# A retention kernel on eight cores: the gated products move from VectorE to GpSimd, the row scale to ScalarE

## The chip, the cores and the metric

The kernel runs on all eight cores of one Trainium2 chip. Each core works on two sequences of its own; the cores exchange nothing. The metric is the device time of the slowest core, in microseconds.

## What is computed

One layer on x of shape 16 x 2048 x 1024. The attention part is a retention with four heads (q and k 256 wide, v 512 wide), with a norm and a gate per head:

```python
xn = layernorm(x)
q, k = rotary(xn @ Wq, xn @ Wk);  v = xn @ Wv          # per head
# per chunk of tokens, gamma per head:
attn  = (q_c @ k_c.T) * decay
o_c   = attn @ v_c + (q_c * cross_q) @ S
S     = gamma**chunk * S + (k_c * cross_k).T @ v_c
o     = o * rsqrt(mean(o*o) + 1e-5) * gn_weight        # per token and head
s     = (o * silu(xn @ Wg)) @ Wo
out   = x + s * silu(ffn(xn))                          # ffn: silu(gate) * up, down
```

The kernel takes chunks of 128 tokens, 16 per sequence.

## The kernel before

For each of its two sequences a core runs two phases with a barrier between them: `_phase_attn` (LayerNorm, and then for each of four heads the projections and the recurrence) and `_phase_wo_ffn` (the product with Wo, then the FFN). Engines have their own instruction streams and wait for each other by counting semaphores (`WG(engine, semaphore, value)`).

**Projections of head h.** TensorE computes q and k (transposed), v, and the gate, in 48 groups of eight matmuls; ScalarE evacuates each group (`eraw`, `vtb`, and for the gate a Silu into `gtmp`); VectorE does the rotary products and multiplies the gate by the norm's weight into `ggb` (L508), 16 slots of 512 columns, one per chunk. GpSimd issues the 16 loads of the head's v and gate weights; it waits only for the matmuls of the head before, so they run under that head's recurrence.

**Recurrence of head h**, loop over c = 0 to 15. TensorE's order in a chunk is: `og_tr(c - 5)`, four transposes (L522) of a finished chunk from `og_sb` into the one PSUM tile `ogT_ps`; the matmuls of `o_ps` (L556, and L562 with the state S); two matmuls of the state's increment `U_ps` (L570); then `at_kt(c + 2)`, which computes the scores of chunk c + 2 (L533) and transposes its k (L540) into `kt_ps`. The k transposes wait until `ktok(c + 1)` has been written, by semaphore `sKT`. ScalarE's order is: `og_evac(c - 6)` (L636, `ogT_ps` to `og_st`), `ktok(c)` (L647, `kt_ps` scaled by `ck_sb`), the copy of `o_ps` into `o_win` (L654, four slots), and the square of `o_ps` with its row sum in `ss_sb` (L658). VectorE's order is: the two halves of the S update (L599), the mask of chunk c + 2 (L587), and after every fourth chunk, which ends a window w = c // 4, the norm of the window: eleven small instructions for the rsqrt (L611 and `_quake_rsqrt`, the last is L107) and four products of 128 x 512 (L623) that multiply `o_win` by the row's rsqrt and by `ggb` into `og_sb`. SyncE sends each `og_st` to DRAM.

The first write into a slot of `o_win` in a new window waits for the product that read it:

```python
WG(sc, sOGv.h, b["ogv"] + c - 3)
sc.copy(out=o_win[:, (c % 4) * 512:(c % 4 + 1) * 512],
        in_=o_ps[:, par * 512:(par + 1) * 512]).then_inc(sOE.h, 1)
```

After the loop TensorE does `og_tr` of chunks 11 to 15 and ScalarE `og_evac` of chunks 10 to 15. The next head's first matmul stands behind the last of these transposes in TensorE's stream.

Of the kernel before, what the change touches and what calls it, by code (L numbers as in the profile page):

```python
# [22 lines left out]
NCH = T // CH  # L23
# [89 lines left out]
def build_nc():  # L113
# [40 lines left out]
    rr_sb = A("rr_sb", [128, 4], F32)  # L154
# [170 lines left out]
def _phase_attn(G, s):  # L325
# [26 lines left out]
    o_win = SB("o_win", [128, 4 * 512], BF16)  # L352
    og_sb = SB("og_sb", [128, 4 * 512], BF16)
    og_st = SB("og_st", [128, 2 * 512], BF16)
    sq_scr = SB("sq_scr", [128, 512], F32)
# [9 lines left out]
    with es, nc.Block() as blk:  # L365
# [16 lines left out]

        for h in range(NHEADS):
            b = dict(tp=sTp.n, pe=(b_h0["pe"] if h == 0 else sPE.n), rp=sRP.n,
                     gt=sGT.n,
                     ta=sTa.n, tk=sTk.n, to=sTo.n, tu=sTu.n, tog=sTog.n,
                     at=sAT.n, st=sS.n, rr=sRr.n, ot=sOT.n, ogv=sOGv.n,
                     kt=sKT.n, oe=sOE.n, oge=sOGE.n,
                     sp=[sSPs[0].n, sSPs[1].n])

            @blk.gpsimd
            def _(g, h=h, b=b):
                WG(g, sTp.h, b["tp"])
                for k in range(KC):
                    g.dma_start(out=wv_sb[:, k * 512:(k + 1) * 512],  # L395
                                in_=G.wv_d[k * 128:(k + 1) * 128, h * 512:(h + 1) * 512]
                                ).then_inc(sWH.h, 16)
                    g.dma_start(out=wg_sb[:, k * 512:(k + 1) * 512],
                                in_=G.wgt_d[k * 128:(k + 1) * 128, h * 512:(h + 1) * 512]
                                ).then_inc(sWH.h, 16)  # L400
                sWH.n += 16 * 2 * KC
            wl_h = sWH.n

# [65 lines left out]
            def _(v, h=h, b=b):  # L469
# [36 lines left out]
                for c in range(NCH):  # L506
                    WG(v, sPE.h, b["pe"] + 32 + c + 1)
                    ins = v.tensor_mul(out=ggb[:, c * 512:(c + 1) * 512],  # L508
# [5 lines left out]
            def _(te, h=h, b=b):  # L514
# [33 lines left out]
                for c in range(NCH):  # L548
# [4 lines left out]
                    WG(te, sOE.h, b["oe"] + c - 1)  # L553
                    WG(te, sOT.h, b["ot"] + c - 1)
# [27 lines left out]
            def _(v, h=h, b=b):  # L582
# [11 lines left out]
                for c in range(NCH):  # L594
# [13 lines left out]
                    if c % 4 == 3:  # L608
                        WG(v, sOT.h, b["ot"] + 4 * w + 4)
# [6 lines left out]
                        _quake_rsqrt(v, G.rr_sb[:, 0:4], G.qk3[:, 0:4],  # L616
                                     G.qk1, G.qk2, sem=sRr)
                        v.drain()
                        WG(v, sOE.h, b["oe"] + 4 * w + 4)
                        for cc in range(4):  # L620
                            cw = 4 * w + cc
                            WG(v, sTog.h, b["tog"] + cw - 3)
                            ins = v.scalar_tensor_tensor(  # L623
                                out=og_sb[:, (cw % 4) * 512:(cw % 4 + 1) * 512],
                                in0=o_win[:, cc * 512:(cc + 1) * 512],
                                scalar=G.rr_sb[:, cc:cc + 1],
                                in1=ggb[:, cw * 512:(cw + 1) * 512],
                                op0=ALU.mult, op1=ALU.mult)
                            sOGv.inc(ins)

            @blk.scalar
            def _(sc, h=h, b=b):
# [6 lines left out]

                for c in range(NCH):  # L640
                    par = c % 2
                    w = c // 4
                    if c >= LAG + 1:
                        og_evac(c - LAG - 1)
# [8 lines left out]
                    WG(sc, sOGv.h, b["ogv"] + c - 3)  # L653
                    sc.copy(out=o_win[:, (c % 4) * 512:(c % 4 + 1) * 512],  # L654
# [3 lines left out]
                    sc.activation(out=sq_scr[:, :],  # L658
# [4 lines left out]
                                  ).then_inc(sOT.h, 1)  # L663
                    sOT.n += 1
# [4 lines left out]
            def _(sy, h=h, b=b):  # L669
# [7 lines left out]
                if h == H - 1:  # L677
                    WG(sy, sSPs[0].h, sSPs[0].n)
                    WG(sy, sSPs[1].h, sSPs[1].n)

# [300 lines left out]
```

## Time and profile before

| | us |
|---|---|
| median of 3 runs (2972.0 to 2981.34) | 2979.19 |
| the profiled execution | 2977.59 |
| its span, slowest core (core 0) | 2975.8 |
| spans of the eight cores | 2946.6 to 2975.8 |
| TensorE matmuls busy | 2346.8 (79%) |
| VectorE busy | 804.6 (27%) |
| ScalarE busy | 804.5 (27%) |
| GpSimd busy | 295.2 (10%) |

The profile is that of the slowest core in one execution. The span goes from its first to its last instruction; what lies around it makes the difference to the execution's time. Busy shares are averages over phases of different kinds: in the FFN TensorE is nearly always busy, in the recurrences every engine waits for others. A row's bracket tells how long the engine had been idle before the instruction and what released it. The granted clock is that of TensorE as a share of 2.4 GHz; it has two levels, 1.2 and 2.4 GHz.

### The profile page before, as it was taken

The page shows a single profiled execution, that of the slowest core. Times are in us where ns is not written, and L with a number is a line of the kernel's source. Part 1 is how long each engine was busy: PE and PEld are TensorE (multiplying, and loading weights), DVE is VectorE, ACT ScalarE, POOL GpSimd, SP SyncE. Part 2 cuts the span into 40 slices and gives each one's busy share as a digit, 9 for nine tenths or more (in the row PEclk, how much of TensorE's full clock was granted, in tenths as well). Part 3 has the DMA queues.
Part 4 walks back from the last instruction along what each step waited for, and adds up shares of the span by engine and source line. Part 5 has one row for each costly group of instructions (what it writes and reads, how often), then busy time and mean ns, then how long its engine had stood idle before and what let it go on. Part 6 is the DMA issues. An engine that isn't in the chain of part 4 may idle for free. (4 is left out here: it accounts for less than half of the span.)

```text
span 2975.8 us, 32058 instructions; the slowest of 8 cores (2946.6 to 2975.8 us)
## 1 busy us (share of the span) xinstructions
PE 2346.8 (79%) x10608; PEld 1039.5 (35%) x10608; DVE 804.6 (27%) x1745; ACT 804.5 (27%) x1560; POOL 295.2 (10%) x436
## 2 busy tenths in 40 slices
PE   1395968778459999999914969697883699999999
PEld 0142423333124444444402424243331244444444
DVE  2325343352300111211223243534423001121112
ACT  2534343333301111111045343434332011111110
POOL 2001010100110221021020100101003002201210
PEclk9597978778679999999956969687785899999999
DMA  9102020200293675475380110202003937755753
GB/s 177 59 1 50 8 41 16 34 24 1 56 184 110 82 74 93 111 78 57 113 176 30 19 39 1 47 11 40 19 4 79 180 113 72 74 96 103 74 50 120
DMA packets 295311, 202.03 MB, mean 68 GB/s; under 512 B 210544, under 2 KB 259824, under 8 KB 295024
## 3 DMA queue, kind: packets, MB, share of 16 engines
q0 software_dynamic: 234240, 96.50, 28.3%
q1 hardware_dynamic: 60912, 103.48, 11.0%
q8 instruction: 92, 1.51, 0.2%
q14 instruction: 67, 0.55, 0.1%
HBM read 254.45 MB, written 41.94 MB: 100 GB/s over the span
## 5 line engine op out<-in xcount | busy, mean ns | idle before, releaser
L842 PE MATMUL P<-xnT,wgu 128*128 128x512 bf16 x1536 | 353.2, 384 | 27.9 <-DMA wgu<-fuw 18.9
L898 DVE TENSOR_TENSOR hT<-sg_sc,P 128x1024 bf16<-128x1024 bf16 x96 | 117.2, 1221 | 923.8 <-PE P L853 923.8
L853 PE MATMUL P<-xnT,wgu 128*128 128x512 bf16 x1536 | 347.2, 379 | 0.0
L869 PE MATMUL P<-wd_sb,hT 128*128 128x512 bf16 x1536 | 332.2, 379 | 6.8 <-DVE hT L898 6.8
L773 PE MATMUL P<-wo_sb,ogl 128*128 128x512 bf16 x1024 | 234.9, 394 | 98.1 <-DMA wo_sb<-wo 72.0
L881 ACT ACTIVATE sg_sc<-P 128x1024 bf16<-128x1024 f32 x96 | 98.3, 1024 | 565.8 <-PE P L842 565.7
L842 PEld LDWEIGHTS P<-xnT,wgu 128*128 128x128 bf16 x1536 | 148.1, 99 | 224.3 <-issue 61.0
L435 PE MATMUL U_ps<-wv_sb,xnT 128*128 128x512 bf16 x1024 | 222.3, 379 | 0.0
L435 PE MATMUL U_ps<-wg_sb,xnT 128*128 128x512 bf16 x1024 | 222.3, 379 | 0.0
L869 PEld LDWEIGHTS P<-wd_sb,hT 128*128 128x128 bf16 x1536 | 150.0, 98 | 188.9 <-issue 8.6
L599 DVE SCALAR_TENSOR_TENSOR S<-S,U_ps 128x512 bf16<-128x512 bf16 x240 | 154.0, 683 | 224.0 <-PE U_ps L570 224.0
L853 PEld LDWEIGHTS P<-xnT,wgu 128*128 128x128 bf16 x1536 | 150.3, 98 | 181.2
L315 PE MATMUL lnps<-id_sb,ln_xn 128*128 128x128 bf16 x256 | 30.3, 291 | 201.6 <-DMA wk_sb<-wk 105.3
L540 PE MATMUL kt_ps<-id_sb,kT 128*128 128x128 bf16 x256 | 43.2, 264 | 182.3 <-ACT ktok L647 182.3
L773 PEld LDWEIGHTS P<-wo_sb,ogl 128*128 128x128 bf16 x1024 | 102.6, 101 | 229.9 <-issue 118.2
L819 POOL DMA_DIRECT2D wgu<-fgw x92 | 80.4, 874 | 966.2 <-PE P L853 966.2
L654 ACT CAST o_win<-o_ps 128x512 bf16<-128x512 f32 x128 | 75.0, 586 | 319.1 <-PE o_ps L562 223.1
L421 PE MATMUL U_ps<-xnT,wq_sb 128*128 128x512 bf16 x512 | 144.9, 453 | 14.3 <-ACT xnT L275 14.3
L508 DVE TENSOR_TENSOR ggb<-gtmp,gw_sb 128x512 bf16<-128x512 bf16 x128 | 54.5, 426 | 373.0 <-ACT gtmp L462 373.0
L435 PEld LDWEIGHTS U_ps<-wg_sb,xnT 128*128 128x128 bf16 x1024 | 100.2, 98 | 120.8
L435 PEld LDWEIGHTS U_ps<-wv_sb,xnT 128*128 128x128 bf16 x1024 | 100.2, 98 | 120.8
L395 POOL DMA_DIRECT2D wv_sb<-wv x64 | 40.4, 631 | 1007.2 <-PE U_ps L435 1007.2
(85 smaller groups left out, 2225.7 us busy)
## 6 DMA issues: line engine op xcount, KB each, us to landing
wgu<-fgw POOLq DMA_DIRECT2D x96, 256.0 KB, 4.7
wgu<-fuw POOLq DMA_DIRECT2D x96, 256.0 KB, 5.3
ln_x<-x SPq DMA_DIRECT2D x32, 512.0 KB, 6.3
og_spill<-og_st SPq DMA_DIRECT2D x128, 128.0 KB, 1.7
ogl<-og_spill SPq DMA_DIRECT2D x128, 128.0 KB, 2.6
xc_sb<-x SPq DMA_DIRECT2D x32, 512.0 KB, 4.0
out<-o_sb SPq DMA_DIRECT2D x32, 512.0 KB, 5.1
wd_sb<-fdw POOLq DMA_DIRECT2D x48, 256.0 KB, 39.5
```

What stands on the lines that cost most here:

```text
L421: ins = te.matmul(U_ps[:, par * 512:(par + 1) * 512], wsb[:, k * D + (2 * h + d) * 128: k * D + (2 * h + d + 1) * 128], G.xnT[:, k * T + n ...
L435: ins = te.matmul(U_ps[:, par * 512:(par + 1) * 512], G.xnT[:, k * T + c * 128:k * T + (c + 1) * 128], wsb[:, k * 512:(k + 1) * 512], star ...
L508: ins = v.tensor_mul(out=ggb[:, c * 512:(c + 1) * 512], in0=gtmp[:, (c % 2) * 512:(c % 2 + 1) * 512], in1=G.gw_sb[:, h * 512:(h + 1) * 512])
L599: ins = v.scalar_tensor_tensor(out=Sb[(c + 1) % 2][:, d * 512:(d + 1) * 512], in0=Sb[c % 2][:, d * 512:(d + 1) * 512], scalar=float(GAMMAS ...
L654: sc.copy(out=o_win[:, (c % 4) * 512:(c % 4 + 1) * 512], in_=o_ps[:, par * 512:(par + 1) * 512]).then_inc(sOE.h, 1)
L773: ins = te.matmul(ps[:, n * 512:(n + 1) * 512], ogl[:, (m % 2) * 2048 + k * 128: (m % 2) * 2048 + (k + 1) * 128], wo_sb[:, k * D + n * 512 ...
L819: g.dma_start(out=wgu[:, par * 1024:(par + 1) * 1024] .rearrange("p (k j) -> p k j", j=128), in_=G.fgw_d[m].rearrange("(k p) j -> p k j", ...
L842: ins = te.matmul(fgps[:, n * 512:(n + 1) * 512], wgu[:, par * 1024 + k * 128: par * 1024 + (k + 1) * 128], G.xnT[:, k * T + tok0 + n * 51 ...
L853: ins = te.matmul(fups[:, n * 512:(n + 1) * 512], wgu[:, 2048 + par * 1024 + k * 128: 2048 + par * 1024 + (k + 1) * 128], G.xnT[:, k * T + ...
L869: ins = te.matmul(ps[:, n * 512:(n + 1) * 512], hT[:, k * 1024 + mc * 128:k * 1024 + (mc + 1) * 128], wd_sb[:, k * D + n * 512:k * D + (n ...
L881: sc.activation(out=sg_sc[:, (m % 2) * 1024:(m % 2 + 1) * 1024], in_=fgps[:, :], func=AF.Silu, scale=Q127).then_inc(sFE.h, 1)
L898: ins = v.tensor_mul(out=hT[:, m * 1024:(m + 1) * 1024], in0=sg_sc[:, (m % 2) * 1024:(m % 2 + 1) * 1024], in1=fups[:, :])
```

## The change

Three things happen to a window's norm. The rsqrt stays on VectorE and now writes one of two halves of `rr_sb`. The multiplication by the row's rsqrt goes to ScalarE: `ot_batch(w)` makes four scaled copies of 128 x 512 from `o_win` into a new tile `ot8`. It stands at the head of chunk 4w + 5, ahead of `og_evac` and `ktok` of that chunk, and for the last window after the loop, ahead of the remaining `og_evac`s. The multiplication by `ggb` goes to GpSimd (`emit_og_gp`), whose products wait for `ot8` and write `og_sb`; in GpSimd's stream they stand behind the weight loads of the next head. `o_win` has six slots instead of four and its copy waits for no product. `sOE` now counts the copy and the square (two per chunk) and `sOT` the scaled copies. The square's scratch output goes to `scr`. VectorE waits before each write of `ggb` for the product of the head before. The capture of the counts `b` moves behind GpSimd's code of the head.

```diff
-    rr_sb = A("rr_sb", [128, 4], F32)
+    rr_sb = A("rr_sb", [128, 8], F32)
...
-    o_win = SB("o_win", [128, 4 * 512], BF16)
+    o_win = SB("o_win", [128, 6 * 512], BF16)
+    ot8 = SB("ot8", [128, 4 * 512], BF16)
...
-    sq_scr = SB("sq_scr", [128, 512], F32)
...
+        def emit_og_gp(g, bo):
+            for j in range(NCH):
+                WG(g, sOT.h, bo["ot"] + j + 1)
+                WG(g, sGT.h, bo["gt"] + j + 1)
+                WG(g, sTog.h, bo["tog"] + j - 3)
+                ins = g.tensor_mul(
+                    out=og_sb[:, (j % 4) * 512:(j % 4 + 1) * 512],
+                    in0=ot8[:, (j % 4) * 512:(j % 4 + 1) * 512],
+                    in1=ggb[:, j * 512:(j + 1) * 512])
+                sOGv.inc(ins)
...
                 sWH.n += 16 * 2 * KC
+                if bprev is not None:
+                    emit_og_gp(g, bprev)
...
                     WG(v, sPE.h, b["pe"] + 32 + c + 1)
+                    WG(v, sOGv.h, b["ogv"] + c - 15)
...
-                    WG(te, sOE.h, b["oe"] + c - 1)
-                    WG(te, sOT.h, b["ot"] + c - 1)
+                    WG(te, sOE.h, b["oe"] + 2 * c - 2)
...
-                        WG(v, sOT.h, b["ot"] + 4 * w + 4)
+                        WG(v, sOE.h, b["oe"] + 8 * w + 8)
+                        WG(v, sOT.h, b["ot"] + 4 * w - 4)
...
-                        _quake_rsqrt(v, G.rr_sb[:, 0:4], G.qk3[:, 0:4],
-                                     G.qk1, G.qk2, sem=sRr)
-                        v.drain()
-                        WG(v, sOE.h, b["oe"] + 4 * w + 4)
-                        for cc in range(4):
-                            cw = 4 * w + cc
-                            WG(v, sTog.h, b["tog"] + cw - 3)
-                            ins = v.scalar_tensor_tensor(
-                                out=og_sb[:, (cw % 4) * 512:(cw % 4 + 1) * 512],
-                                in0=o_win[:, cc * 512:(cc + 1) * 512],
-                                scalar=G.rr_sb[:, cc:cc + 1],
-                                in1=ggb[:, cw * 512:(cw + 1) * 512],
-                                op0=ALU.mult, op1=ALU.mult)
-                            sOGv.inc(ins)
+                        _quake_rsqrt(v, G.rr_sb[:, wp * 4:wp * 4 + 4],
+                                     G.qk3[:, 0:4], G.qk1, G.qk2, sem=sRr)
...
+                def ot_batch(wb):
+                    WG(sc, sRr.h, b["rr"] + wb + 1)
+                    for cc in range(4):
+                        j = 4 * wb + cc
+                        WG(sc, sOGv.h, b["ogv"] + j - 3)
+                        sc.activation(out=ot8[:, (j % 4) * 512:(j % 4 + 1) * 512],
+                                      in_=o_win[:, (j % 6) * 512:(j % 6 + 1) * 512],
+                                      func=AF.Identity,
+                                      scale=G.rr_sb[:, (wb % 2) * 4 + cc:
+                                                    (wb % 2) * 4 + cc + 1]
+                                      ).then_inc(sOT.h, 1)
+                        sOT.n += 1
...
+                    if c % 4 == 1 and c >= 5:
+                        ot_batch(w - 1)
                     if c >= LAG + 1:
                         og_evac(c - LAG - 1)
...
-                    WG(sc, sOGv.h, b["ogv"] + c - 3)
-                    sc.copy(out=o_win[:, (c % 4) * 512:(c % 4 + 1) * 512],
+                    sc.copy(out=o_win[:, (c % 6) * 512:(c % 6 + 1) * 512],
...
-                    sc.activation(out=sq_scr[:, :],
+                    sc.activation(out=scr[:, 0:512],
...
-                                  ).then_inc(sOT.h, 1)
-                    sOT.n += 1
+                                  ).then_inc(sOE.h, 1)
+                    sOE.n += 1
+                ot_batch(NCH // 4 - 1)
                 for c in range(NCH - LAG - 1, NCH):
                     og_evac(c)
...
+            bprev = b
+
+        @blk.gpsimd
+        def _(g, bprev=bprev):
+            emit_og_gp(g, bprev)
```

## Rows read from the trace of the kernel before

**Rows 1.** The profile page, its first line.
```profile
span 2975.8 us, 32058 instructions; the slowest of 8 cores (2946.6 to 2975.8 us)
```

**Rows 2.** The page's chain that ended last: shares of the span by line.
```profile
PE P L869 6%; PE P L842 5%; PE P L853 4%; DMA wgu<-fuw 2%; POOL wgu L819 0%; DVE hT L898 0%; DVE t_sb L906 0%; DVE o_sb L910 0%; ACT g_sc L888 0%; POOLq L42 0%; DVEq L42 0%; ACTq L42 0%; DVEq L909 0%
```

**Rows 3.** Head 1's recurrence, 387-467: PE, PEld, DVE, ACT, POOL busy; PEclk, DMA share, GB/s.
```profile
387.00:467.00 80.00, 47.32 (x206) 19.84 (x204) 41.33 (x108) 33.74 (x80) 7.77 (x15) 0.61 0.27 50
```

**Rows 4.** Timeline, a plain chunk step: start, length, engine, line, [idle before <-releaser].
```profile
416.19 0.59 ACT L654 CAST o_win<-o_ps 128x512 bf16<-128x512 f32 x1 [2.40 <-PE o_ps L562]
...
417.72 0.50 ACT L647 ACTIVATE ktok<-kt_ps,ck_sb 128x256 bf16<-128x256 bf16 x1
...
418.36 0.37 PE L540 MATMUL kt_ps<-id_sb,kT 128*128 128x128 bf16 x2 [1.25 <-ACT ktok L647]
...
418.59 0.58 PE L522 MATMUL ogT_ps<-id_sb,og_sb 128*128 128x128 bf16 x4
...
420.62 0.59 ACT L654 CAST o_win<-o_ps 128x512 bf16<-128x512 f32 x1 [2.41 <-PE o_ps L562]
```

**Rows 5.** Timeline, the same step at the full TensorE clock.
```profile
434.73 0.59 ACT L654 CAST o_win<-o_ps 128x512 bf16<-128x512 f32 x1 [1.77 <-PE o_ps L562]
...
438.53 0.59 ACT L654 CAST o_win<-o_ps 128x512 bf16<-128x512 f32 x1 [1.77 <-PE o_ps L562]
```

**Rows 6.** Timeline, evacuations around the first ends of a window of four.
```profile
397.70 0.59 ACT L654 CAST o_win<-o_ps 128x512 bf16<-128x512 f32 x1 [2.26 <-PE o_ps L562]
...
401.45 0.59 ACT L654 CAST o_win<-o_ps 128x512 bf16<-128x512 f32 x1 [2.21 <-PE o_ps L562]
...
411.76 0.59 ACT L654 CAST o_win<-o_ps 128x512 bf16<-128x512 f32 x1 [3.28 <-PE o_ps L562]
...
426.10 0.59 ACT L654 CAST o_win<-o_ps 128x512 bf16<-128x512 f32 x1 [3.45 <-DVE og_sb L623]
...
430.93 0.59 ACT L654 CAST o_win<-o_ps 128x512 bf16<-128x512 f32 x1 [2.80 <-PE o_ps L562]
...
448.76 0.59 ACT L654 CAST o_win<-o_ps 128x512 bf16<-128x512 f32 x1 [2.79 <-PE o_ps L562]
```

**Rows 7.** Groups by line: busy us, mean ns | idle before, releasers.
```profile
L898 DVE TENSOR_TENSOR hT<-sg_sc,P 128x1024 bf16<-128x1024 bf16 x96 | 117.2, 1221 | 923.8 <-PE P L853 923.8
...
L654 ACT CAST o_win<-o_ps 128x512 bf16<-128x512 f32 x128 | 75.0, 586 | 319.1 <-PE o_ps L562 223.1 <-DVE og_sb L623 87.3 <-PE o_ps L556 8.7
...
L647 ACT ACTIVATE ktok<-kt_ps,ck_sb 128x256 bf16<-128x256 bf16 x128 | 62.7, 490 | 0.1
...
L508 DVE TENSOR_TENSOR ggb<-gtmp,gw_sb 128x512 bf16<-128x512 bf16 x128 | 54.5, 426 | 373.0 <-ACT gtmp L462 373.0
...
L540 PE MATMUL kt_ps<-id_sb,kT 128*128 128x128 bf16 x256 | 43.2, 264 | 182.3 <-ACT ktok L647 182.3
...
L302 ACT ACTIVATE ln_xn<-ln_x,lb_sb,lr_sb 128x1024 bf16<-128x1024 f32 x32 | 37.1, 1230 | 7.9 <-DVE lb_sb L265 7.9
```

**Rows 8.** Timeline of ScalarE in the LayerNorm: four scaled writes in a run.
```profile
132.39 4.63 ACT L302 ACTIVATE ln_xn<-ln_x,lb_sb,lr_sb 128x1024 bf16<-128x1024 f32 x4
```

**Rows 9.** Timeline, end of head 1 and start of head 2.
```profile
457.01 0.59 ACT L654 CAST o_win<-o_ps 128x512 bf16<-128x512 f32 x1 [1.80 <-PE o_ps L562]
...
458.08 0.59 ACT L636 COPY og_st<-ogT_ps 128x512 bf16<-128x512 bf16 x1
...
459.54 0.59 ACT L636 COPY og_st<-ogT_ps 128x512 bf16<-128x512 bf16 x1 [0.88 <-PE ogT_ps L522]
...
460.71 0.16 DVE L107 TENSOR_TENSOR rr_sb<-rr_sb,qk 128x4 f32<-128x4 f32 x1
...
462.16 0.59 PE L522 MATMUL ogT_ps<-id_sb,og_sb 128*128 128x128 bf16 x4 [2.77 <-DVE og_sb L623]
...
466.55 0.58 PE L522 MATMUL ogT_ps<-id_sb,og_sb 128*128 128x128 bf16 x4 [0.88 <-ACT og_st L636]
...
466.93 8.31 PE L421 MATMUL U_ps<-xnT,wq_sb 128*128 128x512 bf16 x25
```

More of the change, by code:

```diff
@@ L381, in _ @@
             sWQK.n += 16 * 2 * KC
-        for h in range(NHEADS):
[L384 to L389, printed above, removed]
+        def emit_og_gp(g, bo):
[8 more added lines that the diff above has]
+                sOGv.inc(ins)
+        bprev = None
+        for h in range(NHEADS):
+            tp_gate = sTp.n
             @blk.gpsimd
-            def _(g, h=h, b=b):
-                WG(g, sTp.h, b["tp"])
+            def _(g, h=h, tp_gate=tp_gate, bprev=bprev):
+                WG(g, sTp.h, tp_gate)
                 for k in range(KC):
@@ L401, in _ @@
                 sWH.n += 16 * 2 * KC
+                if bprev is not None:
+                    emit_og_gp(g, bprev)
             wl_h = sWH.n
+            b = dict(tp=sTp.n, pe=(b_h0["pe"] if h == 0 else sPE.n), rp=sRP.n,
+                     gt=sGT.n,
+                     ta=sTa.n, tk=sTk.n, to=sTo.n, tu=sTu.n, tog=sTog.n,
+                     at=sAT.n, st=sS.n, rr=sRr.n, ot=sOT.n, ogv=sOGv.n,
+                     kt=sKT.n, oe=sOE.n, oge=sOGE.n,
+                     sp=[sSPs[0].n, sSPs[1].n])
             @blk.tensor
```

## The prediction, made before the result was known

> **What bounds the kernel now.** I read the page first. Its span is 2975.8 us [rows 1]; the execution took 2977.59 us, 1.8 us more, and against the median of the runs shown (2979.19 us) it is 0.05% low, so I make the sum on 2977.59. The chain that ended last has only lines of the FFN in it [rows 2]; it does not reach back to the attention phase, where every changed line stands. But each sequence runs its phases one after the other with a barrier between them, and inside the attention phase the recurrence of head h stands before the projections of head h+1 on TensorE. So what the recurrence of one head gains or loses, the total gains or loses, eight times (four heads, two sequences). I read head 1 of the first sequence. In its 80 us TensorE is busy 47.3 us, VectorE 41.3, ScalarE 33.7, GpSimd 7.8, and the granted clock is 0.61 [rows 3]. No engine is full: the recurrence is bound by a loop of waits.
>
> The timeline shows the loop. A plain step, from one `o_win` evacuation to the next, is 4.43 us (416.19 to 420.62) [rows 4]. ScalarE evacuates `o_ps`, squares it, evacuates a transposed chunk (`og_st`) and writes `ktok`, whose start is 1.53 us after the first. TensorE can transpose the next pair of k chunks only when that `ktok` is written (L540 starts at 418.36, after "ACT ktok"), then come `og_tr` (418.59) and the three matmuls of `o_ps`, whose end starts the next evacuation. The grouped row of L540 says the same of all heads: TensorE idles 182.3 us before it, all for `ktok` [rows 7]. So everything that ScalarE does ahead of `ktok` lies on the path, though ScalarE is idle half of the time. At the full clock the step is 3.80 us [rows 5].
>
> Twice per window of four chunks the step is longer. The evacuation of chunk 4w+4 waits for VectorE's products, which free the `o_win` slot (426.10, "DVE og_sb"), and the update of S stands behind these products on VectorE, which makes the step after it long too. For the two steps together I read 401.45 to 411.76 = 10.31 us, 420.62 to 430.93 = 10.31 us and 438.53 to 448.76 = 10.23 us [rows 4 to 6].
>
> **The change, part by part.**
>
> *Products leave VectorE, `o_win` has six slots.* Both waits of these two steps go. Of ScalarE's idle time before L654, 87.3 us is for `og_sb` [rows 7], 24 times (three window ends in eight heads), so 3.64 us each, of which a plain step has 2.40 [rows 4] anyway; the late S makes the step after 4.83 us, not 4.43 [rows 4, 6]. Against plain steps the three pairs are 2.6 us too long (against 3.75 + 3.96, next part), 1.8 and 1.7 (against 2 x 4.27, the mean step, same place): 6.1 us a head, 48 us in all. That is what the change can take away.
>
> *ScalarE gets four scaled copies per window (`ot_batch`).* They stand at the head of chunk 4w+5, before its `og_evac` and its `ktok`. By the loop above TensorE waits for that `ktok`, so the batch lies on the path with its full length. No row shows such a copy. Plain copies of this width take 586 ns and a scaled one of half the width 490 ns; four scaled and biased ones of twice the width take 4.63 us in a run, 1230 ns each, so they start (4.63 - 1.23)/3 = 1.13 us apart and overlap by 0.1 [rows 7, 8]. A copy as fast as a plain one would cost 0.59 - 0.1 = 0.49 us. The line from 490 ns (256 wide) to 1230 ns (1024 wide) gives 0.74 at 512 wide, less the overlap 0.64; that has a bias in it which this copy has not. I take 0.60, so 2.4 us per batch; the ends are 0.49 and 0.64, and 1.13 is the far one. The Trainium skill (ScalarE: Activation LUTs, What ACT_TABLE_LOAD costs) has 186 ns + 0.833 ns per element, 93 ns for each pointer operand and 93 ns of overlap, an estimate of 0.61 us here; by it the sum below would be 1.6 us higher. This case's half-wide scaled copy agrees with it (492 against 490 ns [rows 7]).
>
> *Two steps after the change.* First window: no `og_evac` is due yet, so the steps are 3.75 (397.70 to 401.45 [rows 6]) and 4.43 less the `og_evac`'s 0.47 (3.96), plus 2.4 = 6.36: 10.11 against 10.31, a gain of 0.2 us. The two later window ends: plain + plain + 2.4. At the half clock that is 11.26 us, at the full one 10.0. A granted clock of 0.61 means 22% of the time at 2.4 GHz and the rest at 1.2 GHz [rows 3], about one step in four, so four steps are 3 x 4.43 + 3.80 = 17.09 (4.27 each), and with two batches 21.89, against 10.31 + 10.23 = 20.54: a loss of 1.35 us. Interior of a head: +1.15 us. So 48 us of waits for VectorE are exchanged for 3 x 2.4 x 8 = 58 us of ScalarE.
>
> *The end of a head.* Before, ScalarE's `og_evac` of chunks 10 and 11 (458.08, 459.54) and the transposes between them run while VectorE works out the rsqrt (last instruction 460.71 + 0.16), and transpose 12 starts at 462.16 after the first product [rows 9]. The rest follows 1.46 us apart ((466.55 - 462.16)/3), and the next head's matmuls start at 466.93. After, the last batch stands ahead of `og_evac(10)` and waits for the rsqrt: copies from 460.95 on, `og_evac(10)` at 460.95 + 2.4 = 463.35. From there to transpose 15 it is as it was from 458.08: 0.73 us to transpose 11, then four times 1.46, so 463.35 + 0.73 + 5.84 = 469.92, and the next head starts 0.38 later, at 470.30 instead of 466.93: +3.37 us. This holds while the products keep ahead. The first can start at 460.95 + 0.7 + 0.1 = 461.75, and the fourth has to be done by 469.9: up to 2.04 us each.
>
> *GpSimd's products.* In the interior the first one is due when `og_tr` is ready, 2.4 + 0.47 + 0.5 + 0.4 us after the batch starts, so up to about 2.9 us each is hidden. No row has GpSimd arithmetic. The same product of two bf16 tiles takes VectorE 0.43 us, and its widest product of a tile, twice this width, 1.22 us [rows 7]; I take the upper one, as GpSimd's speed is unknown. Both are under 2.04, so it costs nothing at either end. Its queue: the 16 weight loads of the next head are issued ahead of the products, as before, within the 7.8 us that GpSimd is busy [rows 3], and the first product is due some 19 us into the recurrence. The weights are wanted only after the next head's q and k projections.
>
> *At nothing:* the moved capture of counts, the squares' other scratch tile, the second half of `rr_sb`, and VectorE's new wait before `ggb` (products of a head ago). The rsqrt keeps its place, and S of the next chunk behind it is wanted only after the batch.
>
> **Sum.** Per head -0.2 + 1.35 + 3.37 = +4.5 us; eight heads +36 us: 2977.6 + 36 = 3014 us.
>
> **Rivals.**
>
> *Gains survive because TensorE's clock rises.* Three plain steps now follow each other where there were two, so the granted clock might be full more of the time. If all of it were: three steps of the window ends (1.9 us), three other steps (1.9), the first window's two (1.3), all by 4.43 - 3.80, and some 0.8 at the tail. That is -5.9 us a head, 2967 us, faster. It is level with today once three quarters of the half-clock time has turned (36 of 47 us), and 0.3% faster only with nearly all of it. Against it: each batch leaves TensorE idle 2.4 us longer in one step, and idle stretches of this length stand in the present trace within stretches of the half clock [rows 3, 9]. The other way, all at half clock costs 1.9 us a head more, 3029 us.
>
> *The batch is hidden.* If `ktok` were not what TensorE waits for, the 48 us would be kept and only the tail lost: 2977.6 - 48 + 27 = 2957 us, faster. It turns at 36 of the 58 us hidden. L540's idle time speaks against it [rows 7]. Milder: the copies cost 0.49 us, 128 of them save 14 us, 3000 us.
>
> *GpSimd's product is slow.* Over 2.04 us each further us costs 4 us per tail, 32 us in all: at 3 us it is 3014 + 31 = 3045. For it: no row has arithmetic on GpSimd, so the 1.22 us is VectorE's and not its own. The Trainium skill (GPSIMD Engine Reference, Elementwise — side-by-side cycle accounting) gives 2.6 cycles per element for two inputs at 1.2 GHz, an estimate of 1.1 us here; no row here shows it, and by it this rival does not happen.
>
> **Chances.** About 0.3%, 9 us, is what a measurement of this kernel can tell from no change. Forecast with its clock and copy variants 0.70 (own range 2995 to 3032), slow product 0.12, clock rises fully or the batch is hidden 0.08, something between these and the forecast 0.10, which lies partly within 9 us. So faster 0.08, same 0.10, slower 0.82. For 8 in 10 I go from 2985 (part of the clock's gain or of the hiding) to 3045 (product of 3 us).
>
> **What would show it.** In the changed profile: the o_win evacuation waits for no product; a step with four `ot8` writes of about 0.7 us in 2.4 us, and a step of about 6.8 us around it; TensorE's idle time before L540's successor above 182 us, for `ktok`; the gap from the last `o_win` of a head to the next head's first matmul 13.3 us, not 9.9; GpSimd products under 2 us. I am wrong if `ktok` of chunk 4w+5 does not come later by the batch, if the products pace the last transposes, or if the granted clock in 387 to 467 us leaves 0.55 to 0.70.

## The result and the profile after

The changed kernel takes 2993.29 us (median of 10 runs) against 2978.56 us (median of 11); the ratio is 1.0056, with a 95% interval of 1.0038 to 1.0075. It is slower by about 17 us. The forecast was 3014 us. The sign came true, and the time lies in the range (2985 to 3045), but 36 us had been worked out and less than half of it came; 2993 us is just outside the forecast's own range (2995 to 3032). (Ratios and mean clocks here leave out disturbed runs, in which one die, a group of four cores, ran at a lower clock.)

The page and the grouped rows of the changed kernel, slowest core (core 4); the first line answers to [rows 1], the groups to [rows 7]:

```profile
span 2990.8 us, 32217 instructions; the slowest of 8 cores (2967.3 to 2990.8 us)
...
PE 2298.7 (77%) x10399; PEld 1035.2 (35%) x10608; DVE 719.1 (24%) x1617; ACT 882.9 (30%) x1688; POOL 438.9 (15%) x564
```

```profile
L388 POOL TENSOR_TENSOR og_sb<-ot,ggb 128x512 bf16<-128x512 bf16 x128 | 143.2, 1149 | 609.6 <-ACT ot L650 609.6
...
L650 ACT ACTIVATE ot<-o_win,rr_sb 128x512 bf16<-128x512 bf16 x128 | 81.7, 714 | 24.7 <-DVE rr_sb L107 24.7
...
L673 ACT CAST o_win<-o_ps 128x512 bf16<-128x512 f32 x128 | 74.9, 585 | 242.5 <-PE o_ps L578 226.1 <-remote 8.4 <-PE o_ps L572 8.0
...
L557 PE MATMUL kt_ps<-id_sb,kT 128*128 128x128 bf16 x256 | 41.5, 254 | 206.6 <-ACT ktok L667 206.6
```

GpSimd's products take 1.149 us each, ScalarE's scaled copies 714 ns. Before the copy into `o_win` (L673 now) ScalarE no longer idles for a product (`remote` stands where the profile names no instruction as the releaser); and TensorE's idle time before the k transposes, for `ktok`, has grown from 182.3 to 206.6 us.

The timeline of head 1 around the first window's end, where `ot_batch` stands. Before, the two steps took 10.31 us [rows 6]:

```profile
404.08 0.59 ACT L673 CAST o_win<-o_ps 128x512 bf16<-128x512 f32 x1 [1.47 <-PE o_ps L578]
...
405.43 2.56 ACT L650 ACTIVATE ot<-o_win,rr_sb 128x512 bf16<-128x512 bf16 x4 [0.17 <-DVE rr_sb L107]
...
406.42 4.47 POOL L388 TENSOR_TENSOR og_sb<-ot,ggb 128x512 bf16<-128x512 bf16 x4 [9.90 <-ACT ot L650]
...
407.89 0.46 ACT L667 ACTIVATE ktok<-kt_ps,ck_sb 128x256 bf16<-128x256 bf16 x1
...
408.49 0.27 PE L557 MATMUL kt_ps<-id_sb,kT 128*128 128x128 bf16 x2 [3.96 <-ACT ktok L667]
...
410.68 0.58 ACT L673 CAST o_win<-o_ps 128x512 bf16<-128x512 f32 x1 [2.33 <-PE o_ps L578]
```

Four copies take 2.56 us from the first start to the last end, and their starts are (2.56 - 0.71)/3 = 0.62 us apart, so the batch holds `ktok` up by 4 x 0.62 = 2.5 us; `ktok` starts only behind them (407.89), and TensorE has idled 3.96 us when the k transposes start. The step from copy to copy is 410.68 - 404.08 = 6.60 us; at later window ends, with an `og_evac` in it, it is 6.8. The prediction had named "a step of about 6.8 us".

The end of head 1, which answers to [rows 9]:

```profile
455.22 0.58 ACT L673 CAST o_win<-o_ps 128x512 bf16<-128x512 f32 x1 [1.72 <-remote]
...
458.98 0.16 DVE L107 TENSOR_TENSOR rr_sb<-rr_sb,qk 128x4 f32<-128x4 f32 x1
459.29 2.56 ACT L650 ACTIVATE ot<-o_win,rr_sb 128x512 bf16<-128x512 bf16 x4 [2.90 <-DVE rr_sb L107]
...
461.75 0.56 ACT L641 COPY og_st<-ogT_ps 128x512 bf16<-128x512 bf16 x1
...
462.46 0.59 PE L539 MATMUL ogT_ps<-id_sb,og_sb 128*128 128x128 bf16 x4 [6.48 <-ACT og_st L641]
...
468.30 0.58 PE L539 MATMUL ogT_ps<-id_sb,og_sb 128*128 128x128 bf16 x4 [0.88 <-ACT og_st L641]
...
468.68 6.68 PE L437 MATMUL U_ps<-xnT,wq_sb 128*128 128x512 bf16 x19
```

The last batch waits for the rsqrt (459.29), `og_evac(10)` stands behind it (461.75), and the next head starts 468.68 - 455.22 = 13.46 us after the last `o_win` copy, where it was 9.92. Predicted were 13.3.

The stretch of head 1 whose clock the prediction gave as a sign, in the order of columns of [rows 3]:

```profile
387.00:467.00 80.00, 39.62 (x198) 18.15 (x201) 31.08 (x93) 43.68 (x96) 26.43 (x32) 0.76 0.27 49
```

The granted clock is 0.76 on this core, outside the 0.55 to 0.70 that the prediction allowed. Over the eight cores the same stretch has 0.60 to 0.70 before and 0.65 to 0.76 after.

For what a single place cannot show I took the starts of all 128 `o_win` copies of a core from the timeline and averaged over eight heads and eight cores (the gap over the six on each core that lead to another head). "Plain five" are the steps of a head out of a window's end and with all the work in them (5 to 6, 6 to 7, 9 to 10, 10 to 11, 13 to 14), "full" is their share under 4 us, that is at 2.4 GHz, and the gap goes from a head's last copy to the first of the next.

| us per head | before | predicted change | after | measured change |
|---|---|---|---|---|
| first three steps | 10.85 | 0 | 10.54 | -0.31 |
| two steps at the first window's end | 10.29 | -0.2 | 9.91 | -0.38 |
| four steps at the two later ones | 20.52 | +1.35 | 21.20 | +0.68 |
| plain five | 21.00 (full 0.39) | 0 | 19.91 (full 0.56) | -1.09 |
| last step | 3.67 | 0 | 3.48 | -0.19 |
| gap to the next head | 99.82 | +3.37 | 103.14 | +3.32 |
| sum | 166.14 | +4.5 | 168.18 | +2.04 |

Eight times 2.04 is 16 us, close to the measured 17. The gap came as forecast. What failed is every row of the interior, by the same sign: together they came out 2.4 us a head below the forecast. 1.6 us of it are in steps that the change was not thought to touch, and 0.85 us in the steps at the window ends.

### The profile page after: what moved, and what is told of

The parts are those of the page before. It is cut to its first block and busy times, and to the rows that moved or that the text cites. A ratio compares the mean times of both kernels' runs of the same rounds, so it can differ in the third digit from the quotient of the medians.

```text
span 2990.8 us, 32217 instructions; the slowest of 8 cores (2967.3 to 2990.8 us)
## 1 busy us (share of the span) xinstructions
PE 2298.7 (77%) x10399; PEld 1035.2 (35%) x10608; DVE 719.1 (24%) x1617; ACT 882.9 (30%) x1688; POOL 438.9 (15%) x564
## 5 line engine op out<-in xcount | busy, mean ns | idle before, releaser
L388 POOL TENSOR_TENSOR og_sb<-ot,ggb 128x512 bf16<-128x512 bf16 x128 | 143.2, 1149 | 609.6 <-ACT ot L650 609.6
L557 PE MATMUL kt_ps<-id_sb,kT 128*128 128x128 bf16 x256 | 41.5, 254 | 206.6 <-ACT ktok L667 206.6
L437 PE MATMUL U_ps<-xnT,wq_sb 128*128 128x512 bf16 x497 | 137.5, 440 | 17.5 <-ACT xnT L275 15.0
L673 ACT CAST o_win<-o_ps 128x512 bf16<-128x512 f32 x128 | 74.9, 585 | 242.5 <-PE o_ps L578 226.1
```

What stands on the lines that cost most here:

```text
L388: ins = g.tensor_mul(out=og_sb[:, (j % 4) * 512:(j % 4 + 1) * 512], in0=ot8[:, (j % 4) * 512:(j % 4 + 1) * 512], in1=ggb[:, j * 512:(j + 1 ...
L437: ins = te.matmul(U_ps[:, par * 512:(par + 1) * 512], wsb[:, k * D + (2 * h + d) * 128: k * D + (2 * h + d + 1) * 128], G.xnT[:, k * T + n ...
L673: sc.copy(out=o_win[:, (c % 6) * 512:(c % 6 + 1) * 512], in_=o_ps[:, par * 512:(par + 1) * 512]).then_inc(sOE.h, 1)
```

## Why plain steps are shorter: waits that are always satisfied

Theory W. The diff also takes a wait from each of the two engines of the loop: on TensorE `WG(te, sOT.h, ...)` ahead of the `o_ps` matmuls, on ScalarE `WG(sc, sOGv.h, ...)` ahead of the `o_win` copy. In a plain step both had long been satisfied. Rows of such a place before (core 0) and after (core 4), both at the full clock:

```profile
437.14 0.38 PE L522 MATMUL ogT_ps<-id_sb,og_sb 128*128 128x128 bf16 x4
...
437.58 0.38 PE L556 MATMUL o_ps<-vtb,atm 128*128 128x512 bf16 x1
...
437.79 0.59 PE L562 MATMUL o_ps<-S,qT 128*128 128x512 bf16 x2
```

```profile
428.61 0.58 ACT L673 CAST o_win<-o_ps 128x512 bf16<-128x512 f32 x1 [2.33 <-PE o_ps L578]
...
431.01 0.38 PE L539 MATMUL ogT_ps<-id_sb,og_sb 128*128 128x128 bf16 x4
...
431.39 0.38 PE L572 MATMUL o_ps<-vtb,atm 128*128 128x512 bf16 x1
...
431.60 0.59 PE L578 MATMUL o_ps<-S,qT 128*128 128x512 bf16 x2
...
432.29 0.59 ACT L673 CAST o_win<-o_ps 128x512 bf16<-128x512 f32 x1 [1.65 <-PE o_ps L578]
```

From the transposes of `og_sb` to the first `o_ps` matmul it is 0.44 us before and 0.38 after; from the last pair of `o_ps` matmuls (L562, L578) to the copy 438.53 [rows 5] - 437.79 = 0.74 before and 0.69 after. Theory C, the rival: the steps are shorter because the clock is full more often, and the rows differ by chance.

**Both waits back.** The changed kernel with one satisfied wait more on each engine:

```diff
                     WG(te, sOE.h, b["oe"] + 2 * c - 2)
+                    WG(te, sKT.h, b["kt"] + c)
...
                     WG(sc, sTo.h, b["to"] + c + 1)
+                    WG(sc, sTk.h, b["tk"] + c + 1)
                     sc.copy(out=o_win[:, (c % 6) * 512:(c % 6 + 1) * 512],
```

> The changed kernel with one wait more on TensorE ahead of the o_ps matmuls and one more on ScalarE ahead of the o_win copy, both always satisfied when they are reached, so that each engine has as many waits per chunk as before the change. Theory W (a satisfied wait costs time on the loop): each gives back some 0.07 us, plain steps go from 4.36 and 3.67 to 4.43 and 3.80, first steps from 3.55 to 3.71; 15 steps in eight heads, +8 to +16 us on the changed kernel, ratio to the kernel before about 1.009. Theory C (only the clock made the steps shorter): no change of the steps at equal clock, ratio 1.0056 as the changed kernel.

The ratio to the kernel before is 1.0102 (1.0080 to 1.0124), from two runs of this kernel, so this is some 14 us slower than the change. Its timeline, head 1:

```profile
429.24 0.59 PE L579 MATMUL o_ps<-S,qT 128*128 128x512 bf16 x2
...
429.98 0.59 ACT L675 CAST o_win<-o_ps 128x512 bf16<-128x512 f32 x1 [1.77 <-PE o_ps L579]
...
439.25 0.38 PE L539 MATMUL ogT_ps<-id_sb,og_sb 128*128 128x128 bf16 x4
...
439.70 0.38 PE L573 MATMUL o_ps<-vtb,atm 128*128 128x512 bf16 x1
```

The two distances are 0.74 (429.24 to 429.98) and 0.45 us (439.25 to 439.70) again. The head's steps sum to 67.28 us, the change's to 65.03, and per head this kernel stands 4.6 us above the kernel before (170.75 against 166.14), close to the 4.5 that the prediction had summed up (the ratio gives 3.8). The total agrees better than its rows: the first three steps are 0.38 us above the kernel before, the last step is 0.42 below, the window ends 1.05 above and the gap 3.65.

At equal clock the medians of the plain steps, over all cores and heads, leave the clock out of the comparison:

| us | full clock | half clock |
|---|---|---|
| before | 3.80 | 4.43 |
| after | 3.67 | 4.36 |
| after, both waits back | 3.80 | 4.43 |
| after, TensorE's wait back | 3.75 | 4.38 |
| after, ScalarE's wait back | 3.73 | 4.41 |
| before, one wait fewer on TensorE | 3.72 | 4.42 |

Theory W holds (the last three kernels follow).

**One wait at a time**, one profiled execution each. The same kernel with only TensorE's wait, and with only ScalarE's.

> The changed kernel with the satisfied wait ahead of the o_ps matmuls on TensorE alone. One look: theory W expects about 0.07 us from the og transposes to the o_ps matmuls (0.44 instead of 0.37), plain step at the full clock 3.73, first steps 3.62 to 3.71.

> The changed kernel with the satisfied wait ahead of the o_win copy on ScalarE alone. One look: theory W expects about 0.06 us from the last o_ps matmul to the copy (0.74 instead of 0.68), plain step at the full clock 3.72.

Medians of head 1 on cores 0, 2, 4 and 6, from the timeline, at the full clock: transposes to `o_ps` 0.37 us in the change, 0.44 with TensorE's wait, 0.37 with ScalarE's; last `o_ps` pair to the copy 0.685, 0.68 and 0.74. At the half clock the second distance goes from 1.15 to 1.15 and 1.20. So each wait costs 0.05 to 0.07 us, where it stands.

What the step pays is another matter: ScalarE's wait costs it 0.06 us at the full clock and 0.05 at the half, TensorE's 0.08 at the full and 0.02 at the half. At the half clock the first `o_ps` matmul still comes 0.06 us later with TensorE's wait, but the second hardly (0.82 instead of 0.81 us after the transposes; at the full clock 0.66 instead of 0.58).

The heads' steps sum to 66.59 and 66.50 us, each some 1.5 above the change: more than 15 steps times 0.06 = 0.9. Most of the rest goes with the clock: the share of plain steps at the full clock is 0.41 and 0.43, with both waits 0.42, in the change 0.56 and before 0.39. It is no accident of one core: with both waits the single cores have 0.35 to 0.50, in the change 0.53 to 0.60. In the plain five, 1.04 us separate the kernel with both waits from the change; at a share of 0.41 the change's steps (4.36 and 3.67 us) would sum to 20.4 us, so about half is the waits' own time and half is clock. Why the clock is full more often with them gone is not shown. The other executions have it too: over the whole kernel the granted clock is 0.869 before and 0.875 after, the mean of all cores and runs.

One place of the Trainium skill bears on the size (Advanced Engine Details and Errata, Network/Comms): 50 to 100 ns to read a semaphore's value from a sequencer. The 0.05 to 0.07 us here lie in it; that it is this read that costs was not tested.

**The kernel before with one wait fewer.** Copy and square count on one semaphore, as in the change, so TensorE waits once per chunk. VectorE's two waits at a window's end become one with it, so TensorE's is not quite the only one gone.

```diff
-                    WG(te, sOE.h, b["oe"] + c - 1)
-                    WG(te, sOT.h, b["ot"] + c - 1)
+                    WG(te, sOE.h, b["oe"] + 2 * c - 2)
...
-                                  ).then_inc(sOT.h, 1)
-                    sOT.n += 1
+                                  ).then_inc(sOE.h, 1)
+                    sOE.n += 1
```

> The kernel before with one of TensorE's two waits ahead of the o_ps matmuls removed (copy and square count on one semaphore, as in the change), nothing else. Theory W: -0.07 us in the nine or so steps of a head that VectorE does not set, 72 of them, -5 us, ratio 0.998; plain step at the half clock 4.36 or a little more. Theory C: ratio 1.000, steps of 4.43 and 3.80 as before.

Ratio 0.9953 (0.9929 to 0.9978), 14 us: this part of the diff alone makes the old kernel faster, by more than the 5 us expected. The steps of a head fall from 66.32 to 65.36 us, the gap by 0.17: 9 us in eight heads. The plain step was expected at 4.36 us at the half clock and is 4.42; it is 3.72 instead of 3.80 at the full one. So the change's bookkeeping by itself is worth 9 to 14 us in the old kernel, not much less than the 17 us that the change lost in spite of it.

## Whether the prediction's own terms hold

**The tail.** The same change with the two evacuations that used to run under the rsqrt put back there:

```diff
-                ot_batch(NCH // 4 - 1)
-                for c in range(NCH - LAG - 1, NCH):
+                og_evac(NCH - 6)
+                og_evac(NCH - 5)
+                ot_batch(NCH // 4 - 1)
+                for c in range(NCH - 4, NCH):
                     og_evac(c)
```

> The changed kernel with og_evac of chunks 10 and 11 ahead of the last ot_batch instead of behind it, nothing else. If the prediction's tail term is right (evacuations 10 and 11 and the transposes between them no longer run under the rsqrt), transpose 12 follows the first product at once and the next head starts 2.1 us earlier, the head-to-head gap falls from 103.1 to 101.0 us: 8 x 2.1 = 17 us, ratio to the kernel before 1.000. Rival (GpSimd's products pace the last transposes, 1.12 us each plus the start): the gap stays above 102.5, ratio above 1.003.

```profile
458.47 0.59 ACT L641 COPY og_st<-ogT_ps 128x512 bf16<-128x512 bf16 x1 [0.88 <-PE ogT_ps L539]
...
460.02 2.56 ACT L650 ACTIVATE ot<-o_win,rr_sb 128x512 bf16<-128x512 bf16 x4 [0.96 <-DVE rr_sb L107]
...
462.69 0.59 PE L539 MATMUL ogT_ps<-id_sb,og_sb 128*128 128x128 bf16 x4 [4.37 <-POOL og_sb L388]
...
467.46 2.76 PE L437 MATMUL U_ps<-xnT,wq_sb 128*128 128x512 bf16 x6
```

`og_evac(11)` is done (458.47 + 0.59) before the copies start (460.02), and transpose 12 waits for nothing but GpSimd's first product ("POOL og_sb"). The gap falls from 103.14 to 101.02 us, as expected; the ratio is 1.0014 (0.9993 to 1.0034), 12.5 us less than the change, level with the kernel before. The 17 us expected (eight gaps of 2.1) lie inside the interval. So 2.1 of the 3.3 us are the evacuations' place. The other 1.2 fit the way that a window's first product now takes, over ScalarE's copy and GpSimd: transpose 12 starts 2.7 us after the first copy (460.02 to 462.69), where before it started 1.3 us after the rsqrt's last instruction [rows 9].

**The batch ahead of `ktok`.** Only the first copy stays there; two follow this `ktok`, one the next:

```diff
                     if c % 4 == 1 and c >= 5:
-                        ot_batch(w - 1)
+                        ot_batch(w - 1, (0,))
...
                     sKT.n += 1
+                    if c % 4 == 1 and c >= 5:
+                        ot_batch(w - 1, (1, 2))
+                    if c % 4 == 2 and c >= 5:
+                        ot_batch(w - 1, (3,))
```

> The changed kernel with only the first copy of a batch ahead of ktok of chunk 4w+5; two copies follow that ktok and one follows the next ktok, in the 1.6 to 2.4 us in which ScalarE waits for o_ps. Theory L (copies ahead of ktok lie on the path with their full length): the 6.8 us step falls to about 5.2 us (three copies of 0.64 us less, 0.3 us of new waiting of the first transposes for their product), 24 times 1.6 us = -38 us, ratio to the kernel before 0.993. Rival H (the batch is mostly hidden): the step stays near 6.8 us, ratio 1.0056.

```profile
418.24 0.59 ACT L677 CAST o_win<-o_ps 128x512 bf16<-128x512 f32 x1 [1.77 <-PE o_ps L578]
...
419.30 0.72 ACT L650 ACTIVATE ot<-o_win,rr_sb 128x512 bf16<-128x512 bf16 x1
...
420.38 0.49 ACT L667 ACTIVATE ktok<-kt_ps,ck_sb 128x256 bf16<-128x256 bf16 x1
...
421.69 0.38 PE L539 MATMUL ogT_ps<-id_sb,og_sb 128*128 128x128 bf16 x4 [0.40 <-POOL og_sb L388]
...
423.65 0.59 ACT L677 CAST o_win<-o_ps 128x512 bf16<-128x512 f32 x1 [1.56 <-PE o_ps L578]
```

The step is 5.41 us (418.24 to 423.65) instead of 6.80: `ktok` starts at 420.38, and the og transposes now wait 0.40 us for their product. The ratio is 0.9936 (0.9918 to 0.9954). The mean over cores and heads falls from 6.80 to 5.2 us, three copies of 0.62 less that wait, as expected. So the copies lay on the path with their full length, and the same ScalarE work placed behind `ktok` makes the change faster than the kernel before.

**Both.**

> The changed kernel with both rearrangements, the split batch and the two evacuations ahead of the last batch. If the two lie on the path independently, their gains add: head's steps 60.6 us as with the split alone, gap 101.1 us as with the tail alone; ratio to the kernel before 0.9936 - 0.0042 = 0.989 to 0.990. Rival (the split's new waits or the products eat the tail's gain): 0.992 or more.

Ratio 0.991 (0.988 to 0.9939), an interval that holds the expectation and its rival both; the trace tells them apart. The gap is 101.11 us as with the tail alone, but the steps sum to 61.93 us, not 60.66. The steps at the window ends are as short as with the split alone; the plain five are 21.11 us instead of 19.79, with a share at the full clock of 0.20 instead of 0.58. The gains added where they were made, and 1.3 us a head went back by the clock. All executions show it: the granted clock over the whole kernel is 0.871, with the split alone 0.883. What lowered it is open.

**GpSimd's product twice.** Every product is made twice, the first into an idle tile.

```diff
+                g.tensor_mul(
+                    out=xn_sb[:, (j % 4) * 512:(j % 4 + 1) * 512],
+                    in0=ot8[:, (j % 4) * 512:(j % 4 + 1) * 512],
+                    in1=ggb[:, j * 512:(j + 1) * 512])
                 ins = g.tensor_mul(
```

> The changed kernel in which GpSimd makes every product twice (the first into an idle tile), so 2.3 us per chunk instead of 1.15. By the prediction's bounds (hidden up to 2.9 us in the interior, up to 2.04 us at the end of a head) the steps inside a head stay (65.0 us) and the gap from head to head grows: the fourth product ends at about 9.2 us after the first begins, 1.4 us after transpose 15 starts now; gap 104.5, +11 us, ratio to the kernel before 1.009 to 1.010. Rival S (GpSimd slows VectorE or ScalarE while it reads): the steps inside a head grow too, S updates of 684 ns get longer, ratio above 1.015.

```profile
471.51 0.59 PE L543 MATMUL ogT_ps<-id_sb,og_sb 128*128 128x128 bf16 x4 [1.26 <-POOL og_sb L392]
...
472.32 1.15 POOL L392 TENSOR_TENSOR og_sb<-ot,ggb 128x512 bf16<-128x512 bf16 x1
...
473.73 0.59 PE L543 MATMUL ogT_ps<-id_sb,og_sb 128*128 128x128 bf16 x4 [1.63 <-POOL og_sb L392]
```

Only at the end of a head do the products pace the transposes (473.73, 1.63 us for "POOL og_sb"). The gap is 104.39, the steps 65.29 us against 65.03, ratio 1.0098 (1.0062 to 1.0134). Both bounds of the prediction, 2.9 us in the interior and 2.04 at the tail, fit this: 2.3 us lies between them, was hidden in the interior and was not at the tail. The S update, which reads one tile from SBUF (S) and one from PSUM (`U_ps`), takes 684 ns with GpSimd busy twice as long, 684 ns in the change, and 683 before, without any product on GpSimd. The rule of the Trainium skill agrees (SBUF — State Buffer, Who interferes with whom): a VectorE instruction with at most one SBUF input, outside the two-port modes, does not contend with GpSimd.

## What the change was to take away

**`o_win` alone.** The kernel before with eight slots, so that no copy waits for a product; the products stay on VectorE.

```diff
-    o_win = SB("o_win", [128, 4 * 512], BF16)
+    o_win = SB("o_win", [128, 8 * 512], BF16)
...
-                    WG(sc, sOGv.h, b["ogv"] + c - 3)
+                    WG(sc, sOGv.h, b["ogv"] + c - 7)
```

> The kernel before with eight slots of o_win, so that its copy waits for no product, and the products still on VectorE. Theory D (what costs in a window's end is the S update behind the products; the copy's wait is the same time seen on another engine): the step into chunk 4w+4 falls by about 1 to 1.6 us, the next grows by nearly as much, since o_ps of chunk 4w+5 waits for S; the pair stays within 0.3 us of 10.3, ratio 0.998 to 1.000. Rival E (the copy's wait is a cost of its own): the pair falls by 1.2 us, 24 times, -30 us, ratio 0.990.

```profile
422.88 0.59 ACT L654 CAST o_win<-o_ps 128x512 bf16<-128x512 f32 x1 [1.77 <-PE o_ps L562]
...
423.72 2.74 DVE L623 SCALAR_TENSOR_TENSOR og_sb<-o_win,rr_sb,ggb 128x512 bf16<-128x512 bf16 x4 [0.29 <-ACT o_win L654]
...
426.38 1.28 DVE L599 SCALAR_TENSOR_TENSOR S<-S,U_ps 128x512 bf16<-128x512 bf16 x2
...
427.81 0.59 PE L556 MATMUL o_ps<-vtb,atm 128*128 128x512 bf16 x1 [2.14 <-DVE S L599]
...
429.39 0.59 ACT L654 CAST o_win<-o_ps 128x512 bf16<-128x512 f32 x1 [4.49 <-PE o_ps L562]
```

The copy at 422.88 waits for no product any more, and the step before it is short. But S of the next chunk stands behind the products on VectorE (426.38), the `o_ps` matmuls wait 2.14 us for it, and this step is 429.39 - 422.88 = 6.51 us. The two pairs at the later window ends sum to 20.50 us, before 20.52. Ratio 1.0012 (0.9995 to 1.0029), where 0.998 to 1.000 was expected and 0.990 by the rival: the profile's 87.3 us of "og_sb" before L654 [rows 7] was worth nothing by itself. The other steps were slower here, with a share at the full clock of 0.12.

**The versions that beat both.** If transposes of finished chunks come six chunks late (`LAG = 6`), no copy has to stand ahead of `ktok`: two follow `ktok` of chunk 4w+5, two that of 4w+6, and evacuations 9 to 11 stand ahead of the last batch.

```diff
-LAG = 5
+LAG = 6
...
-                    if c % 4 == 1 and c >= 5:
-                        ot_batch(w - 1)
...
                     sKT.n += 1
+                    if c % 4 == 1 and c >= 5:
+                        ot_batch(w - 1, (0, 1))
+                    if c % 4 == 2 and c >= 5:
+                        ot_batch(w - 1, (2, 3))
...
+                for c in range(NCH - LAG - 1, NCH - 4):
+                    og_evac(c)
                 ot_batch(NCH // 4 - 1)
```

> The changed kernel with transposes of finished chunks six chunks late instead of five, so that no copy has to stand ahead of ktok: two copies follow ktok of chunk 4w+5, two that of chunk 4w+6, and evacuations 9 to 11 stand ahead of the last batch. Theory L: the copies are hidden fully while ScalarE waits for o_ps; the 6.8 us steps become plain ones of 3.7 to 4.4 us, head's steps about 56.5 us, gap 101.5: per head 8.2 us less than before, 66 us, ratio 0.978. Rival: the two copies (1.3 us) delay o_win copies or the products delay the transposes, head's steps stay above 59 us, ratio above 0.985.

```profile
400.66 0.59 ACT L675 CAST o_win<-o_ps 128x512 bf16<-128x512 f32 x1 [1.14 <-PE o_ps L578]
...
401.73 0.48 ACT L665 ACTIVATE ktok<-kt_ps,ck_sb 128x256 bf16<-128x256 bf16 x1
402.08 1.34 ACT L650 ACTIVATE ot<-o_win,rr_sb 128x512 bf16<-128x512 bf16 x2
...
402.35 0.37 PE L557 MATMUL kt_ps<-id_sb,kT 128*128 128x128 bf16 x2 [0.71 <-ACT ktok L665]
...
404.54 0.59 ACT L675 CAST o_win<-o_ps 128x512 bf16<-128x512 f32 x1 [1.11 <-PE o_ps L578]
```

The copies run (402.08) while TensorE goes on with the k transposes (402.35), and the step is 3.88 us. The steps of a head sum to 55.94 us, ten less than before, the gap is 101.26. 2904.36 us (median of 5), ratio 0.9741 (0.9715 to 0.9767), a little more than the 0.978 expected. The plain five are 19.16 us, with a share at the full clock of 0.78, against 19.91 and 0.56 in the change.

The same without ScalarE's waits that repeat an earlier one (the excerpt shows the one ahead of the square; the ones within a group of copies go too):

```diff
-                    WG(sc, sRr.h, b["rr"] + w - 1)
+                    if c % 4 == 0:
+                        WG(sc, sRr.h, b["rr"] + w - 1)
```

> The version with the copies behind ktok and transposes six chunks late, less the waits of ScalarE that repeat an earlier one: the one ahead of the square in three of four chunks, and those within a group of copies. Theory W, if a satisfied wait costs wherever it stands on the path: some 0.03 to 0.07 us in three of four steps, 3 to 6 us, ratio to the kernel before 0.972. If it costs only where the instruction behind it has nothing to overlap with (the square starts 0.48 us after the copy either way): 0.974, as without.

Ratio 0.9771 (0.9713 to 0.9829), an interval too wide to tell it from 0.9741. The steps sum to 55.77 against 55.94 us: if anything is gained it is 0.2 us a head. The square starts before the copy ahead of it has ended (401.14 for 400.66 + 0.59), so it may be that a wait between them is covered; the 0.2 us are too little to show it.

Last, the question whether the other engines are needed at all. The kernel before, its products on VectorE as they were, but two per chunk behind the S update and the mask of chunks 4w+5 and 4w+6, with `LAG = 6`, eight `o_win` slots and the one wait on TensorE:

```diff
-                        for cc in range(4):
-                            cw = 4 * w + cc
...
+                    if c % 4 == 1 and c >= 5:
+                        products(w - 1, (0, 1))
+                    if c % 4 == 2 and c >= 5:
+                        products(w - 1, (2, 3))
+                products(NCH // 4 - 1, (0, 1, 2, 3))
```

> The kernel before with its products still on VectorE, but two per chunk, behind the S update and the mask of chunks 4w+5 and 4w+6, transposes of finished chunks six chunks late, eight slots of o_win, and one wait on TensorE fewer. Theory P (the place of the products costs, not the engine that makes them): two products of 0.75 us fit beside 1.56 us of S update and mask in a step of 3.7 us, the pairs at a window's end fall from 10.3 to about 7.8 us, head's steps about 56 us, and the gap stays at 99.9 since no copy stands at a head's end; ratio 0.971 to 0.975. Rival (VectorE is too full for them and the other engines are needed): head's steps above 59 us, ratio above 0.985.

```profile
412.81 1.28 DVE L610 SCALAR_TENSOR_TENSOR S<-S,U_ps 128x512 bf16<-128x512 bf16 x2 [1.72 <-PE U_ps L569]
...
414.01 0.28 DVE L586 TENSOR_TENSOR atm<-at_ps,dp_sb 128x128 bf16<-128x128 f32 x1
...
414.22 1.40 DVE L595 SCALAR_TENSOR_TENSOR og_sb<-o_win,rr_sb,ggb 128x512 bf16<-128x512 bf16 x2
```

Two products take 1.40 us behind S and the mask, in time in which VectorE waited. Ratio 0.976 (0.9729 to 0.979), 2909.51 us. The pairs at the window ends sum to 7.47 and 15.73 us (before 10.29 and 20.52), the gap is 99.66. The expectation of 56 us for the head's steps was too low, they are 58.47. Against the version with three engines (55.94), the plain five make 1.9 of the 2.5 us (21.06, share 0.45, against 19.16 and 0.78), and the clock explains 0.33 x 0.69 x 5 = 1.1 of that. The rest is not clock. In the steps 5 to 6, 9 to 10 and 13 to 14 the og transposes start 0.4 to 1.1 us after the k transposes instead of 0.23, since the first of the two products comes just ahead of them; such a step at the half clock takes 4.6 to 4.8 us instead of 4.42. And this version keeps ScalarE's satisfied wait, 0.3 us in five steps. The interval overlaps that of the version with three engines: which is faster is not settled.

## Why the prediction was right and where it failed

- **Which loop bounds, and that work ahead of `ktok` lies on it**: right. The batch of four starts holds `ktok` up by 2.5 us (2.4 predicted) and the step around it is 6.80 us (6.8 predicted); moved behind `ktok` its cost went. The Trainium skill's 0.61 us per copy (ScalarE: Activation LUTs, What ACT_TABLE_LOAD costs) was nearer than my 0.60; measured 0.62.
- **The tail**, +3.37 us: measured +3.32, of which putting the evacuations back returned 2.1.
- **GpSimd's product** under 2.04 us: 1.15, so nothing; that the bound lies below 2.3 is shown. Of the Trainium skill's 2.6 cycles per element (GPSIMD Engine Reference, Elementwise — side-by-side cycle accounting) the estimate was 1.1.
- **The step that failed** is "Two steps after the change", with its "plain + plain + 2.4", and with it the list "At nothing". It took plain steps of the new kernel to be those of the old (4.43 and 3.80 us; 3.75 in the beginning) and left out the two waits that the diff removes from the loop. They are 4.36, 3.67 and 3.55. With the waits back the prediction's sum comes out (+4.6 us a head against +4.5), though partly by rows that cancel; without them it is +2.04. The missing term is 2.4 us a head, 20 us. In the plain five about half of it is the waits themselves, and half the clock, whose cause is open.
- **The clock** was held at one step in four. That was read from 80 us of one core, the end of the head included; over all heads and cores 0.39 of the plain steps were at the full clock already before. It moved with the change to 0.56, in the direction of the rival "TensorE's clock rises", though far from deciding. One of the prediction's signs of being wrong came with it: the granted clock of 387 to 467 us left 0.55 to 0.70 (0.76 on the slowest core). The other signs came as forecast.
- **The range** held partly by luck. Its lower end allowed for "part of the clock's gain", which came, but the other part of the gap to 3014 us was a term that the prediction had at nothing.
- **The rival of the hidden batch** did not come true as the change stood, and did in the version with `LAG = 6`.

## What to carry to other kernels

Before costing an operation, find the instruction behind it that the loop waits for: the same four copies cost 2.5 us a window ahead of `ktok` and next to nothing behind it, and VectorE could have kept its products if they had been spread. A wait that the profile charges to one engine can be the same time as a wait on another; lifting it moves the time (eight `o_win` slots: ratio 1.0012). And in a loop of waits between engines, count the waits themselves, satisfied ones too: one fewer on TensorE per 3.7 to 4.4 us step gave 0.5%. What one is worth depends on what else bounds the step: the same wait was 0.08 us of a step at the full clock and 0.02 at the half.

## What the runs showed of the hardware

- A wait that is always satisfied costs 0.05 to 0.07 us where it stands alone on the path, on TensorE and on ScalarE. Of the whole step ScalarE's cost 0.05 to 0.06 us, TensorE's 0.08 at the full clock and 0.02 at the half. Ahead of the square, which overlaps its predecessor, no cost could be told.
- GpSimd multiplies two bf16 tiles of 128 x 512 in 1.15 us, 1.11 us apart in a run ((4.47 - 1.15)/3), without slowing VectorE's S updates (684 ns, before 683).
- The share of a recurrence at the full clock ranged from 0.12 to 0.78 of the plain steps among these kernels, which all do the same matmuls. Each point of 0.1 is worth 0.1 x 0.69 x 5 = 0.35 us a head in the plain five. It went up in the version with the shortest stalls, but not in step with each kernel's idle time (split and tail together: 0.20); what sets it here is open.
